# Macaron block on one core: three score banks, fewer feed-forwards ahead, second feed-forwards later

## The reference

```python
x = x + 0.5 * ffn(layernorm(x))     # "norm1", first feed-forward
x = x + attention(layernorm(x))     # "norm2": 16 heads of 16, rotary embedding, causal
x = x + 0.5 * ffn(layernorm(x))     # "norm3", second feed-forward
# ffn(y) = (silu(y @ up) * (y @ gate)) @ down, 1024 hidden units; the three weights are
#          ternary: clip(round(w / mean|w|), -1, 1) * mean|w|
# attention: softmax(q k^T / 4 + causal mask) v, then @ wo
```

## Time and profile before

| | |
|---|---|
| median of the runs | 728.42 us |
| the profiled execution's own time | 730.72 us |
| its span in the trace | 728.9 us |
| busy: PE, ACT, DVE, POOL | 84%, 82%, 79%, 73% |
| mean granted clock of PE | 0.956 |
| slots 0 to 127 (first row maximum to last exponential) | 87.9 to 688.7 us |

### The profile page before, as it was taken

The page is one execution under the profiler, slowest core; times in us unless marked ns, Lnnn a source line. Parts: engine busy times, 40 slices in busy tenths (PEclk is TensorE's granted clock), DMA queues, the critical chain, the costliest instruction groups (busy, mean ns, idle before and its releaser), DMA issues. The chain is left out here.

```text
span 728.9 us, 16671 instructions
## 1 busy us (share of the span) xinstructions
PE 614.3 (84%) x5961; PEld 471.2 (65%) x5961; DVE 573.4 (79%) x1496; ACT 598.0 (82%) x1179; POOL 530.4 (73%) x533
## 2 busy tenths in 40 slices
PE   1779988969999999999998989899868787876756
PEld 0557766747767777777776868777646464645544
DVE  3886678978989898988888889898868686867633
ACT  4255689879999999999999999999888888877822
POOL 1346588777988888888888897978777677765512
PEclk9999999989999999999999999999999898979877
DMA  9600548486859676868678596859586949596510
GB/s 339 177 14 1 89 73 157 77 172 83 173 87 156 122 139 128 134 130 133 144 107 163 103 160 99 167 89 177 94 183 96 180 94 182 96 180 102 110 36 15
DMA packets 311570, 90.42 MB, mean 124 GB/s; under 512 B 301760, under 2 KB 310208, under 8 KB 311488
## 3 DMA queue, kind: packets, MB, share of 16 engines
q1 hardware_dynamic: 310624, 87.06, 64.3%
q10 hardware_dynamic: 864, 2.29, 0.9%
HBM read 9.63 MB, written 4.19 MB: 19 GB/s over the span
## 5 line engine op out<-in xcount | busy, mean ns | idle before, releaser
L1071 POOL TENSOR_TENSOR hid_l<-hid,hid_h 128x512 f16<-128x512 f32 x128 | 149.3, 1167 | 121.4 <-ACT hid_h L691 119.2
L671 ACT ACTIVATE prob<-score_ps,exp_bias,exp_scale 128x256 f32<-128x256 f32 (+1 forms) x512 | 223.2, 509 | 7.8 <-DVE exp_bias L927 7.4
L1066 POOL TENSOR_TENSOR prob_hl<-prob,prob_hl 128x768 f16<-128x768 f32 x128 | 210.5, 1645 | 20.5 <-ACT prob_hl L682 20.2
L405 PE MATMUL down_ps<-tern_down,hid_h 128*128 128x256 f16 x512 | 121.2, 277 | 21.6 <-POOL hid_l L1071 18.8
L405 PE MATMUL up_ps<-xt_hi,tern_up 128*128 128x256 f16 x512 | 127.7, 286 | 6.8 <-DVE tern_up L777 4.5
L405 PE MATMUL up_ps<-xt_lo,tern_up 128*128 128x256 f16 x512 | 127.6, 286 | 0.0
L405 PE MATMUL gate_ps<-xt_hi,tern_gate 128*128 128x256 f16 x512 | 123.6, 280 | 3.7 <-DVE tern_gate L777 2.1
L686 ACT ACTIVATE tanh_b<-up_ps,tanh_scale 128x512 f32<-128x512 f32 x128 | 87.5, 684 | 45.8 <-PE up_ps L405 42.5
L405 PE MATMUL gate_ps<-xt_lo,tern_gate 128*128 128x256 f16 x512 | 123.2, 280 | 0.0
L920 DVE TENSOR_REDUCE score_ps<-score_ps 128x2 f32<-128x512 f32 x128 | 88.5, 692 | 42.1 <-PE score_ps L432 41.8
L405 PE MATMUL down_ps<-tern_down,hid_l 128*128 128x256 f16 x512 | 121.0, 276 | 0.0
(11 more groups left out here) (104 smaller groups left out, 1331.7 us busy)
## 6 DMA issues: line engine op xcount, KB each, us to landing
xs<-x SPq DMA_DIRECT2D x16, 256.0 KB, 2.9
out<-xs SPq DMA_DIRECT2D x16, 256.0 KB, 2.6
raw_w<-prob_hl SPq DMA_TRANSPOSE x128, 3.8
raw_up<-w_up_t ACTq DMA_DIRECT2D x1, 512.0 KB, 5.3
raw_up<-w_up_t SPq DMA_DIRECT2D x1, 512.0 KB, 5.8
raw_gate<-w_gate_t ACTq DMA_DIRECT2D x1, 512.0 KB, 7.4
raw_gate<-w_gate_t SPq DMA_DIRECT2D x1, 512.0 KB, 7.9
raw_down<-w_down_t ACTq DMA_DIRECT2D x1, 512.0 KB, 8.9
```

What stands on the lines that cost most here:

```text
L405: mm = pe.matmul(dst, lhs, rhs, start=flags and n == 0, stop=n == len(pairs) - 1, skip_group_check=True)
L671: e = act.activation(prob[:, n % 2, at + j * width:at + (j + 1) * width], score_ps[:, 1 - tile, j * width:(j + 1) * width], ACT.Exp, bias= ...
L1066: pool.tensor_tensor(prob_hl[:, n % 2, 1, :], prob[:, n % 2, :], prob_hl[:, n % 2, 0, :], ALU.subtract).then_inc(prob_l_done, 1)
L1071: pool.tensor_tensor(hid_l[:, n % 2, :, :].rearrange("p m n -> p (m n)"), hid[:, n % 2, :], hid_h[:, n % 2, :, :].rearrange("p m n -> p (m ...
```

## The change

- **Rounds.** AHEAD is 4 in place of 7: the first feed-forwards of batches 0 to 3 stand in slots -16 to -1, of b >= 4 at 8(b-4)+6. The second feed-forward of batch b, and norm3 with it, stand four slots later (at 8b+18), but for the last batch (8b+14). Full slots are now 6 to 9 and 14 to 101 without a break, then 106 to 109, 114 to 117 and 122 to 125: 104; pair-only slots 24 (0 to 5, 10 to 13, 102 to 105, 110 to 113, 118 to 121, 126, 127). After slot 127 stand eight rounds: 130 to 137.
- **PSUM.** score_ps has three banks: two for the second rows by the parity of the pair, one for the first rows and the maxima. up_ps has one.
- **Order.** The lists of PE, DVE, ACT, POOL and SP are in another order; scores and row maxima are split in two. v moves from -4 to -3, out_proj from place a to b, the second tile's rope_add and rope_hi one slot later, both row_lo one earlier.
- **Norms.** The variance's epsilon is added on POOL, inside norm_power, in place of DVE; the factor X_SCALE moves into the high and low parts. New leads. xt_hi and xt_lo of norm3 have two buffers, in the memory of raw_up. stats, mean and power wait for the readers of what they overwrite.
- **Start.** The weight sums, maxima, powers and splits stand one to three slots earlier.

```diff
-AHEAD = 7
+AHEAD = 4
-FFN1_AT = 18
+FFN1_AT = 6
+def delay(b):
+    return 4 if b < NBATCH - 1 else 0
-    plan += [(SLOTS * b + FFN2_AT + r, 2, b, r) ...
+    plan += [(SLOTS * b + FFN2_AT + delay(b) + r, 2, b, r) ...
-SUM_GATE_AT, SPLIT_HI_AT, MAXIMA_AT, TOPS_AT, POWERS_AT, SPLIT_LO_AT = FIRST_FFN + (0, 5, 2, 3, 4, 6)
+SUM_GATE_AT, SPLIT_HI_AT, MAXIMA_AT, TOPS_AT, POWERS_AT, SPLIT_LO_AT = FIRST_FFN + (-3, 4, 0, 1, 2, 4)
-PE_DOWN_AT, PE_TURN_AT, PE_SPREAD_AT = FIRST_FFN + (1, 3, 4)
+PE_DOWN_AT, PE_TURN_AT, PE_SPREAD_AT = FIRST_FFN + (0, 1, 2)
-    1: {"stats": 4, "mean": 3, "var": 3, "power": 3, "shift": 2, "apply": 1},
-    2: {"stats": 3, "mean": 3, "var": 2, "power": 2, "shift": 2, "apply": 1},
-    3: {"stats": 2, "mean": 1, "var": 1, "power": 1, "shift": 1, "apply": 0},
+    1: {"stats": 4, "mean": 4, "var": 8, "power": 4, "shift": 4, "apply": 3},
+    2: {"stats": 3, "mean": 3, "var": 0, "power": 3, "shift": 3, "apply": 1},
+    3: {"stats": 1, "mean": 1, "var": 20, "power": 2, "shift": 2, "apply": 1},
-ROPE_ADD, ROPE_HI, ROW_LO = {-7: 0, -6: 1}, {-6: 0, -5: 1}, {-5: 0, -3: 1}
+ROPE_ADD, ROPE_HI, ROW_LO = {-7: 0, -5: 1}, {-6: 0, -4: 1}, {-6: 0, -4: 1}
...
-        up_ps = ps("up_ps", [P, 2, 512])
+        up_ps = ps("up_ps", [P, 512])
-        score_ps = ps("score_ps", [P, 2, 512])
+        score_ps = ps("score_ps", [P, 3, 512])
...
+            def scores_1(n):                # second rows, bank n % 2
+                if n >= 2:
+                    pe.wait_ge(exp_done[0], n - 1)
+            def scores_0(n):                # first rows, bank 2
+                pe.wait_ge(exp_done[1], n)
             def up(n, f, b, r):
-                if n >= 2:
-                    pe.wait_ge(silu_done, n - 1)
+                pe.wait_ge(silu_done, n)
...
             def norm_power(k, b):           # POOL
+                pool.wait_ge(mean_done[k], 2 * (b + 1))
+                pool.tensor_scalar(var_s[k][:, :, None], mv[k][:, :, 1:2], LN_EPS, None, ALU.add).then_inc(var_done[k], 1)
                 pool.wait_ge(var_done[k], b + 1)
```

The lists for g >= 0, written as sequences:

```diff
 PE
-  product_v(g-3), scores(g), misc a, up, gate, misc b, down(g-1)
+  scores_1(g), scores_0(g), misc a, up, product_v(g-3), gate, misc b, down(g-1)
 ACT
-  prob_hi(g-1), rope_hi, misc a, tanh, norm_apply, exps(g, second rows), misc b, exps(g, first rows), hidden_hi
+  misc a, prob_hi(g-1), rope_hi, tanh, norm_apply, exps(g, first rows), misc b, exps(g, second rows), hidden_hi
 DVE
-  ffn_added, pv_inverse(g-3), row_max(g), pv_scale, exp_biases, misc a, stats, pv_add, silu, mean, hidden, var, misc b
+  ffn_added, stats, row_max_0(g), mean, row_max_1(g), misc a, pv_inverse(g-3), exp_biases, pv_scale, pv_add, silu, hidden, misc b
 POOL
-  prob_lo(g-1), rope_add, power, row_lo, shift, hidden_lo
+  rope_add, prob_lo(g-1), power, row_lo, shift, hidden_lo
 SP
-  turn_rows(g), turn_probs(g), store
+  turn_probs(g-1), turn_rows(g), store
```

More of the change, by code:

```diff
@@ L89, in plan_rounds @@
     plan += [(SLOTS * (b - AHEAD) + FFN1_AT + r, 1, b, r) for b in range(AHEAD, NBATCH) for r in range(ROUNDS)]
-    plan += [(SLOTS * b + FFN2_AT + r, 2, b, r) for b in range(NBATCH) for r in range(ROUNDS)]
+    plan += [(SLOTS * b + FFN2_AT + delay(b) + r, 2, b, r) for b in range(NBATCH) for r in range(ROUNDS)]
     return sorted(plan)
@@ L98 @@
 FFN_ADD = {FFN_START[f, b] + ROUNDS + 1: (f, b) for f, b in FFN_ORDER}
-OF_BATCH = [("norm2", -8, "a"), ("qk0", -8, "b"), ("qk1", -6, "a"), ("v", -4, "b"),
-            ("attn_t", 10, "b"), ("out_proj", 11, "a"), ("norm3", 13, "b")]
-MISC = sorted([(SLOTS * b + at, place, what, b) for what, at, place in OF_BATCH for b in range(NBATCH)] +
+OF_BATCH = [("norm2", -8, "a"), ("qk0", -8, "b"), ("qk1", -6, "a"), ("v", -3, "b"),
+            ("attn_t", 10, "b"), ("out_proj", 11, "b"), ("norm3", 13, "b")]
+MISC = sorted([(SLOTS * b + at + (delay(b) if what == "norm3" else 0), place, what, b) for what, at, place in OF_BATCH for b in range(NBATCH)] +
               [(FFN_START[1, b] - 1, "a", "norm1", b) for b in range(NBATCH)])
@@ L256, in macaron_kernel @@
         v_row = sb("v_row", [P, 2, NT * HEADS, VW], F16)
-        exp_bias = sb("exp_bias", [P, 4])
+        exp_bias = sb("exp_bias", [P, 2, 4])
         prob = sb("prob", [P, 2, 6 * P])
@@ L388, in slot @@
             def slot(g):
+                for n in pair_of(g, 1):
+                    turn_probs(n)
                 for b, tile in events(g, ROW_LO):
                     turn_rows(b, tile)
-                for n in pair_of(g, 0):
-                    turn_probs(n)
                 if g in FFN_ADD:
@@ L410, in three, with masked_scores @@
                 return [(a_hi, b_hi), (a_hi, b_lo), (a_lo, b_hi)]
-            def scores(n):
+            def masked_scores(dst, q, k):
+                pe.matmul(dst[:, :, -P:], ident_b[:, :], mask_b[:, :].rearrange("p (j n) -> p j n", j=2),
+                          start=True, stop=False, skip_group_check=True)
+                return pe.matmul(dst, q, k, start=False, stop=True, skip_group_check=True)
+            def scores_1(n):
                 b, s = divmod(n, SLOTS)
@@ L560, in slot @@
                         up(*r)
+                    for r in round_of(g, 0):
+                        gate(*r)
+                    for n in pair_of(g, 0):
+                        scores_0(n)
+                    for name, b in uses_of(g, "b"):
+                        misc(name, b)
+                    for n in pair_of(g, 0):
+                        scores_1(n)
+                    for r in round_of(g, 1):
+                        down(*r)
+                else:
+                    for n in pair_of(g, 0):
+                        scores_1(n)
+                    for n in pair_of(g, 0):
+                        scores_0(n)
+                    for name, b in uses_of(g, "a"):
+                        misc(name, b)
+                    for r in round_of(g, 0):
+                        up(*r)
+                    for n in pair_of(g, 3):
+                        product_v(n)
                     for r in round_of(g, 0):
@@ L671, in exps @@
                     e = act.activation(prob[:, n % 2, at + j * width:at + (j + 1) * width],
-                                       score_ps[:, 1 - tile, j * width:(j + 1) * width], ACT.Exp,
-                                       bias=exp_bias[:, bias:bias + 1], scale=exp_scale[:, :])
+                                       score_ps[:, n % 2 if tile else 2, j * width:(j + 1) * width], ACT.Exp,
+                                       bias=exp_bias[:, n % 2, bias:bias + 1], scale=exp_scale[:, :])
                 e.then_inc(exp_done[1 - tile], 1)
@@ L702, in slot @@
                 if g < 0:
[L703 to L723, removed]
                     for b, tile in events(g, ROPE_HI):
@@ L729, in slot @@
                         tanh(n)
+                    for name, b in uses_of(g, "b"):
+                        misc(name, b)
+                    for k, b in norms(g, "apply"):
+                        norm_apply(k, b)
+                    for n in round_numbers(g, 0):
+                        hidden_hi(n)
+                    for n in pair_of(g, 0):
+                        exps(n, 0)
+                    for n in pair_of(g, 0):
+                        exps(n, 1)
+                    for n in pair_of(g, 1):
+                        prob_hi(n)
+                else:
+                    for name, b in uses_of(g, "a"):
+                        misc(name, b)
+                    for n in pair_of(g, 1):
+                        prob_hi(n)
+                    for b, tile in events(g, ROPE_HI):
+                        rope_hi(b, tile)
+                    for n in round_numbers(g, 0):
+                        tanh(n)
                     for k, b in norms(g, "apply"):
@@ L732, in slot @@
                     for n in pair_of(g, 0):
-                        exps(n, 1)
+                        exps(n, 0)
                     for name, b in uses_of(g, "b"):
@@ L736, in slot @@
                     for n in pair_of(g, 0):
-                        exps(n, 0)
+                        exps(n, 1)
                     for n in round_numbers(g, 0):
@@ L967, in slot @@
                 if g < 0:
-                    for n in pair_of(g, 3):
-                        pv_inverse(n)
                     if g in FFN_ADD:
@@ L984, in slot @@
                     for n in pair_of(g, 3):
-                        pv_add(n)
+                        pv_inverse(n)
+                    for n in pair_of(g, 3):
+                        pv_scale(n)
+                    for n in round_numbers(g, 0):
+                        silu(n)
                     for n in round_numbers(g, 0):
                         hidden(n)
-                    for n in pair_of(g, 0):
-                        exp_biases(n)
                     for name, b in uses_of(g, "b"):
@@ L992, in slot @@
                     for n in pair_of(g, 0):
-                        row_max(n)
+                        exp_biases(n)
```

(14 more changed lines are left out.)

165 lines of the change are left out of this document (69 added, 96 removed).

## The result

The changed kernel takes 717.87 us (median of four runs, 715.55 to 720.52) against 728.34 for the kernel before on the same chip: a ratio of 0.9852 (0.9825 to 0.9879), 1.5% faster. The forecast was 706 us. The profiled run took 718.6 us with a span of 716.7.

What follows compares the result with a forecast made beforehand. ACT and PE, within 5% of the period, bound full slots; a chain of waits bound pair-only stretches. 87.9 start + 576.7 slots (104 x 4.68 + 24 x 3.75) + 42 end = 706.6, less 0.5: 706 us, range 690 to 726.

Steps and rivals of the forecast that it cites:

- Start: Before slot 0: same DVE instructions in another order, taken as 0 us change, bounds -3 and +3.
- End: From the last exponentials to the end: 42 us in place of 40.2, bounds 39 and 45.
- Full slots: 104 slots with a round: 37.4 us a batch, 4.68 a slot, against 4.76 before.
- the 36.3: ACT's busy time per batch of full slots, taken as an unchanged floor: 36.3 us, 4.54 a slot.
- I take 3.75 each: The 24 pair-only slots: 3.75 us each against 4.36 before, bounds 3.1 and 4.36.
- stepping: Working engine lists through slot by slot with estimated durations; gave 13.4 to 14 us per four late pair-only slots.
- the second rival: No slot gains: in pair-only slots the DMA or PE at its lower clock level binds; 729 us, 8%.
- 0.5 under: Correction from forecast span to run time: 0.5 us taken off 706.6, giving 706.
- the variance: 48 instructions moved from DVE to POOL: priced at no period change, since DVE is not the bound.
- The check on the kernel before: Slot prices 106 x 4.76 + 22 x 4.36 = 600.5 us, against 600.8 measured in the kernel before.
- First rival (in step): Full slots keep ACT and PE in step at 4.76 or more, only pair-only slots gain; 714 us, 20%.
- Slower rival: The bias stands behind the product on DVE, ACT waits 0.9 us a slot; half the full slots give 753 us; 8%.

Runs made afterwards that it cites:

- e3: Changed kernel plus eight filler matmuls of 256 columns at PE's end of each of the 24 pair-only slots; 712.2 us (0.9767).
- e7: e3 with three buffers instead of two for both the split and the transposed probabilities; 710.39 us (0.974).
- e6: Changed kernel with the second rows' scores of pair n waiting for exps n-1 instead of n-2, as with a single bank; 793.93 us (1.0888).
- e10: Changed kernel with the 48 variance instructions back on DVE, between row_max_1 and batch work a; 728.71 us (1.0006).
- e1: Changed kernel (new lists, banks and norms) with the old distribution of rounds; 767.97 us (1.0528 to the kernel before).
- e2: Kernel before (old lists) with only the new distribution of rounds; 762.42 us (1.045).
- e8: e1 with v one slot earlier, at -4 as in the kernel before; 746.39 us (1.0242 to the kernel before).
- e5: Changed kernel with product_v moved back ahead of batch work a and up in PE's list, slots from 0 on; 730.16 us (1.0022).

## Why the prediction was wrong

- *Direction and most terms held.* Start: 0 was said, -1.6 measured, no more than chance: the changed kernel, e3 and e7 share this start, and their first maxima begin at 86.3, 85.2 and 87.1. End: 42 said, 42.5 measured, by the chain described. Full slots: 4.68 said; slots 16 to 95 take 377.0 us from bias to bias, 4.71 a slot (+3 us over 104). ACT's busy time there fell to 35.87 a batch with the same instructions, so the 36.3 was no floor, and the stalls were larger than the sum had them: 1.7 us a batch (37.6 less 35.87), not 1.1. The loop left behind was PE in step with ACT; e6 shows that the bank is what breaks it.
- *The step that failed is "I take 3.75 each" for pair-only slots.* The slots took 587.9 us; less 104 x 4.71 = 489.8 that leaves 98.1 / 24 = 4.09 each, 8 us over the 90 forecast. By the same count, which is an estimate, the ten opening ones took 4.4 each and the fourteen late ones 3.8, where stepping gave 3.35 to 3.5 for late ones. The dearest stretch is the four intervals between biases from slot 110 on: 5.01, 4.61, 5.16 and 5.20, 20.0 us. In e3 and e7 they take 17.9, so the clock explains only part of this stretch.
- *What stood in its place.* The stepping used durations at 2.4 GHz throughout. The new rounds put both emptier stretches where norm2, q/k 0 and norm3 stand; PE, with little between, was granted 0.60 to 0.81, a q/k product took 2.5 us and DVE's rotary product, and the maxima and bias behind it, waited. I had this in the second rival, but only as an all-or-nothing case. Keeping PE busy (e3) gives 5.7 of the 8 us back, and that is shown clear of noise; the third buffers may give 1.8 more. In e7 the slots take 578.9 us, and so (578.9 - 489.8) / 24 = 3.7 each. That this meets the 3.75 on the mean is in part luck: the opening ones are still at 4.0 and the late ones at 3.6, and the dearest stretch is not what was stepped.
- *The rest.* 1.7 us is the run's median standing 1.2 over the profiled span, where I had taken 0.5 under.
- *Priced at nothing for a wrong reason: the variance.* I read the one blocked instance, and concluded that DVE is not the bound. But where DVE's list stands in front of the bias, a hold there reaches ACT, whatever DVE's total load: e10 loses 10.8 us. The price of nothing for the move itself is not refuted, since at its old place the instruction was hardly held in full slots; the reason given for it is.
- *Slot prices by kind.* The check on the kernel before (600.5 against 600.8) looked like a proof of the method. It was not: with the same numbers of slots of each kind, e1 and e2 came out over 50 and over 30 us above their forecasts. A slot's price hangs on which batch work stands in it, on each engine's list, as e8 shows for one slot.
- *First rival (in step):* its 714 us is nearer the time than mine, but its mechanism is not what the trace shows; full slots did gain. *Slower rival:* ACT's wait for the bias is 14.7 us in the whole run and 0.4 in a batch of full slots (bias 64 to bias 72), so it does not bind them. e5, which undoes that order, is 12 us slower, but by another wait, the DMA's.

## What to carry to other kernels

When engines are balanced within 5%, work out the list in front of each cross-engine handover, not the load: an instruction of 0.16 us took 0.87 there. When a schedule is made emptier in one place, look which matmuls will be waited for there and price them at the lower clock level too. An order and the distribution of its work are one edit; here either half alone cost three to four times what both gained.

## What was not expected of the hardware

- 48 VectorE instructions of two columns, placed between a maximum and a bias, cost 10.8 us; one that took 0.16 us elsewhere took 0.87 beside POOL's, and up to 1.175. On POOL they take 0.23 each.
- Eight idle-time matmuls per emptier slot raised the mean clock from 0.951 to 0.982 and gave 5.7 us; sixteen gave the same clock and were 3.8 us slower than none.
- The same filler in the kernel before raised the clock nearly as much (0.956 to 0.980) and gave nothing in time.
